# An attention and expert-layer kernel: w_out transposed by DMA, and the softmax reciprocal taken before its broadcast

## The chip, the cores and the metric

The kernel runs on one Trainium2 chip, on all eight of its cores, one launch. Each core takes one of eight sequences and does the same work on it; the cores exchange nothing. The metric is the device time in microseconds (us) of the slowest core.

## The reference, cut to what matters

For each sequence, x is 2048 x 1024. It is normalised, and two branches read the result: attention with 16 heads of 64 under a causal mask, and four expert layers of which each token takes two. Both are added to x. The change touches attention alone:

```python
xn = _layernorm(x, axis=-1)
qkv = jnp.einsum('bse,fe->bsf', xn, w_qkv)          # w_qkv: 3072 x 1024
scores = jnp.einsum('bhqd,bhkd->bhqk', q, k) * scale
scores = jnp.where(causal, scores, -1e30)
attn = jax.nn.softmax(scores, axis=-1)
out = jnp.einsum('bhqk,bhkd->bhqd', attn, v)
out = out.transpose(0, 2, 1, 3).reshape(B, S, E)
a = jnp.einsum('bse,fe->bsf', out, w_out)           # w_out: 1024 x 1024
y = x + a + experts(xn)
```

The sum in the softmax is divided out last: the kernel computes exp(score - 8) without normalising, multiplies by V extended by a column of ones, so that the 65th row of the result is the sum, and then multiplies the other 64 rows by the reciprocal of that row.

## The kernel before

The program is written engine by engine with semaphores set by hand. `I(engine, semaphore, fn)` adds an instruction that raises a semaphore, `E` one that doesn't, and `W` a wait; each engine runs its own list in the order in which the code emits it. `P.brk()` closes a block: all engines meet at a barrier there. Ahead of the first block proper stand small loads and constants; then come four blocks.

**Block with layernorm, Q, K and V (from L249).** GpSimd waits until two quarters of x have landed and then issues three DMA transfers (L253) that read w_qkv in thirds, K first, cast it to bf16 and write it to `wqkv_bf` in DRAM; nothing waits between them. SyncE loads x in four quarters (L331) and then issues 24 DMA transposes (L339), 128 rows each, from `wqkv_bf` to `wqkvT`; the first of each eight waits for its third's cast (SCB1, SCB0, SCB2), and each waits for the transpose before it (SQT). VectorE and ScalarE do layernorm by quarters (`emit_ln`), TensorE transposes the normalised x (L409) and does Q, K (`emit_qk_tt`, L270) and V (`emit_v`, L304). The first K matmul waits for the first transpose.

**Attention block (from L508).** First w_out: for each of eight groups of 128 rows SyncE loads it in f32 (L514), TensorE transposes eight 128x128 tiles (L521), and VectorE copies each to `w_outT` in bf16 (L526). On ScalarE 16 small activations give the gates of the experts (L534); VectorE finishes the gates (L538 to L548) behind its 64 copies, TensorE transposes them (L556), VectorE copies the results (L559), and the first score matmul waits for the last of these copies.

Then the loop over four query tiles `qt` of 512 rows, and in each over eight head pairs. Tile `qt` has `npair` = 2, 4, 6 or 8 steps; a step p of one head is 256 keys:

- `emit_pair`: two score matmuls (L648, L654) into P45 or P67, Exp over both (L662) into `p_sb`, and in the last two steps of a head a mask multiply on VectorE (L670);
- `emit_av`: two matmuls of `p_sb` with V (L683, L690) that add into one of three PSUM slots. The first of a head waits until the multiply with the reciprocal has freed its slot.

The normalising of a head is put off. `flush_stage1` (L609) copies the sum row out of PSUM after a pair's last step. `flush_stage2` has the rest: a matmul with 64 ones broadcasts the row over 64 partitions into `RBP` (L619), ScalarE takes Ln (L623) and Exp of the negative (L627), and VectorE multiplies into `attn_cat` (L633). For the first head of a pair ("the younger head" in the text, of the pair just finished) stage 2 is emitted in the next pair's loop, right behind the first `emit_av`:

```python
            for p in range(npair):
                emit_av(qt, h0, p, npair, u0, s0, a0)
                if p == 0 and pending[0] is not None:
                    flush_stage2(pending[0])
                if p + 1 < npair:
                    emit_pair(qt, h0, p + 1, npair, u0, s0)
                emit_av(qt, h1, p, npair, u1, s1_, a1)
```

For the second head of a pair it is emitted only after the next pair's loop ("the older head"). So at a change of head pair TensorE has, in order: last `emit_av`, the older head's broadcast, two `emit_pair`, `emit_av` of the first head, the younger head's broadcast, `emit_pair`, `emit_av` of the second head. At the end of a tile both heads of the last pair are flushed one after the other. The out-projection of a tile (L715, L720) is spread over the next tile's first head pair; only it reads `w_outT`. Its result goes by way of `proj` to `attn_sc` (L728, L735). In the last tile GpSimd loads expert weights: one load after the fourth head pair, three more (L579, L571, L579) after the last `emit_av`.

**Expert block** (`emit_h` L814, `emit_y` L843): matmuls 128x512 without a gap. **Last block**: x, the attention result and the expert sum are added and stored.

## Time and profile before

| | us |
|---|---|
| median of three runs (3300.23, 3302.22, 3564.77) | 3302.22 |
| the profiled execution | 3302.43 |
| its span, slowest core (the eight: 3288.4 to 3300.9) | 3300.9 |
| block with layernorm, Q, K, V ends | 368 |
| first score matmul | 404.2 |
| expert layers start | 1298.3 |
| TensorE busy | 2867.4 (87%) |
| ScalarE busy | 861.1 (26%) |
| VectorE busy | 752.0 (23%) |

The span is from the first to the last instruction on the slowest core; the execution's own time is 1.5 us longer. In the rows PE is TensorE's matmul, PEld its weight load, ACT ScalarE, DVE VectorE, POOL GpSimd, and SP or SPq SyncE and its DMA queue.
### The profile page before, as it was taken

The page shows a single profiled execution, that of the slowest core. Times are in us where ns is not written, and L with a number is a line of the kernel's source. Part 1 is how long each engine was busy: PE and PEld are TensorE (multiplying, and loading weights), DVE is VectorE, ACT ScalarE, POOL GpSimd, SP SyncE. Part 2 cuts the span into 40 slices and gives each one's busy share as a digit, 9 for nine tenths or more (in the row PEclk, how much of TensorE's full clock was granted, in tenths as well). Part 3 has the DMA queues.
Part 4 walks back from the last instruction along what each step waited for, and adds up shares of the span by engine and source line. Part 5 has one row for each costly group of instructions (what it writes and reads, how often), then busy time and mean ns, then how long its engine had stood idle before and what let it go on. Part 6 is the DMA issues. An engine that isn't in the chain of part 4 may idle for free. (4 is left out here: it accounts for less than half of the span.)

```text
span 3300.9 us, 30637 instructions; the slowest of 8 cores (3288.4 to 3300.9 us)
## 1 busy us (share of the span) xinstructions
PE 2867.4 (87%) x11396; PEld 1146.4 (35%) x11396; DVE 752.0 (23%) x1048; ACT 861.1 (26%) x1164; POOL 35.2 (1%) x59
## 2 busy tenths in 40 slices
PE   3689757778878885999999999999999999999970
PEld 2364301111111112444444444444444444444420
DVE  4521432221121111111111111111111121111224
ACT  1122144545545552112222111112222211211100
POOL 0000000000000000000000000000000000000000
PEclk9769756565565557999999999999999999999955
DMA  9400100000000106032033123303321330230017
GB/s 157 89 10 1 52 0 26 1 26 0 0 26 0 26 0 102 1 51 40 12 52 52 16 36 51 52 1 52 52 29 23 52 52 7 45 51 1 1 49 256
DMA packets 72295, 127.89 MB, mean 39 GB/s; under 512 B 27798, under 2 KB 27926, under 8 KB 71962
## 3 DMA queue, kind: packets, MB, share of 16 engines
q0 software_dynamic: 33520, 73.40, 15.4%
q1 hardware_dynamic: 38634, 52.53, 5.1%
q8 instruction: 98, 1.61, 0.2%
q14 instruction: 43, 0.35, 0.0%
HBM read 176.26 MB, written 23.07 MB: 60 GB/s over the span
## 5 line engine op out<-in xcount | busy, mean ns | idle before, releaser
L814 PE MATMUL P<-xn_fm,w1g 128*128 128x512 bf16 x4096 | 896.9, 380 | 27.6 <-PEq L43 27.6
L843 PE MATMUL P<-w2g,h_sb 128*128 128x512 bf16 x4096 | 894.3, 379 | 0.0
L822 ACT ACTIVATE h_sb<-P,b_sb 128x512 bf16<-128x512 f32 x512 | 352.4, 688 | 1444.9 <-PE P L814 1444.9
L862 DVE SCALAR_TENSOR_TENSOR accum<-P,agate,accum 128x1024 f32<-128x1024 f32 x240 | 308.1, 1284 | 1379.8 <-PE P L843 1379.8
L814 PEld LDWEIGHTS P<-xn_fm,w1g 128*128 128x128 bf16 x4096 | 400.1, 98 | 515.8 <-issue 37.9
L843 PEld LDWEIGHTS P<-w2g,h_sb 128*128 128x128 bf16 x4096 | 400.7, 98 | 483.4
L662 ACT ACTIVATE p_sb<-P,cneg 128x1024 bf16<-128x1024 f32 x320 | 352.0, 1110 | 324.5 <-PE P L654 324.1
L683 PE MATMUL P<-p_sb,v_ext 128*65 128x512 bf16 x320 | 191.6, 599 | 153.4 <-DVE p_sb L670 69.5
L690 PE MATMUL P<-p_sb,v_ext 128*65 128x512 bf16 x320 | 194.8, 609 | 0.0
L683 PEld LDWEIGHTS P<-p_sb,v_ext 128*65 128x65 bf16 x320 | 41.1, 128 | 408.7 <-issue 407.3
L670 DVE TENSOR_TENSOR p_sb<-p_sb,masks 128x1024 bf16<-128x1024 bf16 x128 | 87.9, 690 | 407.1 <-ACT p_sb L662 407.1
L654 PE MATMUL P<-q_fm,k_fm 64*128 64x512 bf16 x320 | 175.7, 609 | 0.0
L648 PE MATMUL P<-q_fm,k_fm 64*128 64x512 bf16 x320 | 168.6, 583 | 7.2 <-DVE proj L728 6.5
L270 PE MATMUL P<-xn_fm,wqkvT 128*128 128x512 bf16 x448 | 117.2, 405 | 25.8 <-DMA wqkvT<-wqkv_bf 16.4
L648 PEld LDWEIGHTS P<-q_fm,k_fm 64*128 64x128 bf16 x320 | 29.0, 99 | 208.6 <-issue 208.6
L633 DVE TENSOR_TENSOR attn_cat<-P,rb 64x512 bf16<-64x512 f32 x64 | 43.7, 683 | 179.1 <-ACT rb L627 173.7
L409 PE MATMUL P<-ident,xnf 128*128 128x128 f32 x128 | 34.4, 406 | 47.3 <-ACT xnf L400 44.9
L270 PEld LDWEIGHTS P<-xn_fm,wqkvT 128*128 128x128 bf16 x448 | 45.5, 103 | 86.3 <-issue 40.7
L715 PE MATMUL P<-w_outT,attn_cat 128*128 128x512 bf16 x240 | 64.8, 431 | 10.4 <-ACT p_sb L662 7.9
L623 ACT ACTIVATE rln<-P 64x512 f32<-64x512 f32 x64 | 37.8, 591 | 120.8 <-PE P L619 120.2
L438 PE MATMUL P<-wr_sb,xfm 128*128 128x4 f32 x256 | 53.0, 339 | 13.8 <-DVE xfm L428 13.8
L438 PEld LDWEIGHTS P<-wr_sb,xfm 128*128 128x128 f32 x256 | 52.0, 310 | 17.7 <-issue 17.7
(106 smaller groups left out, 1019.4 us busy)
## 6 DMA issues: line engine op xcount, KB each, us to landing
w1g<-w POOLq DMA_DIRECT2D x16, 2048.0 KB, 19.5
w2g<-w POOLq DMA_DIRECT2D x16, 2048.0 KB, 30.2
xA<-x SPq DMA_DIRECT2D x4, 2048.0 KB, 31.6
attn_sc<-proj SPq DMA_DIRECT2D x16, 512.0 KB, 2.8
xrg<-x SPq DMA_DIRECT2D x4, 2048.0 KB, 10.8
arg<-attn_sc SPq DMA_DIRECT2D x4, 2048.0 KB, 16.0
y<-outr SPq DMA_DIRECT2D x16, 512.0 KB, 2.8
wqkv_bf<-w_qkv POOLq DMA_DIRECT2D x3, 2048.0 KB, 43.6
```

The source lines that it names most:

```text
L270: t.matmul(pt[:, off:off + 512], wqkvT[:, dc * 3072 + fc8 * 128:dc * 3072 + (fc8 + 1) * 128], xn_fm[:, dc * 2048 + tt * 512:dc * 2048 + (t ...
L438: E("tensor", lambda t, dc=dc, trp=trp: t.matmul(trp[:, 0:4], xfm[:, dc * 128:(dc + 1) * 128], wr_sb[:, dc * 4:(dc + 1) * 4], start=(dc == ...
L648: E("tensor", lambda t, kb0=kb0, pb=pb, hr=hr, pair=pair, qt=qt: t.matmul(pb[:, 0:512], k_fm[hr:hr + 64, pair * 2048 + kb0 * 128:pair * 20 ...
L654: t.matmul(pb[:, 512:1024], k_fm[hr:hr + 64, pair * 2048 + (kb0 + 1) * 128:pair * 2048 + (kb0 + 2) * 128], q_fm[hr:hr + 64, pair * 2048 + ...
L662: ve = I("scalar", "SS", lambda s, pb=pb, psb=psb: s.activation(psb[:], pb[:, 0:1024], AF.Exp, bias=cneg8[:, 0:1]))
L670: vm = I("vector", "SV", lambda v, psb=psb, j=j: v.tensor_tensor(psb[:], psb[:], masks[:, j * 1024:(j + 1) * 1024], ALU.mult))
L683: E("tensor", lambda t, p=p, head=head, psb=psb, sl=sl: t.matmul(sl[0:65, :], bass.AP(v_ext, 2 * p * VW + head * 65, [[NTS * VW, 128], [1, ...
L690: psb=psb, sl=sl, av_stop=av_stop: t.matmul(sl[0:65, :], bass.AP(v_ext, (2 * p + 1) * VW + head * 65, [[NTS * VW, 128], [1, 65]]), psb[:, ...
L814: t.matmul(PH67[par][:, 0:512], w1g[buf][:, dc * 1024 + hc * 128:dc * 1024 + (hc + 1) * 128], xn_fm[:, dc * 2048 + tt * 512:dc * 2048 + (t ...
L822: s.activation(h_sb[tt % 2][:, hc * 512:(hc + 1) * 512], PH67[par][:, 0:512], AF.Gelu, bias=b1_sb[:, e_ * 32 + g_ * 8 + hc:e_ * 32 + g_ * ...
L843: pt=pt, st=st, sp=sp: t.matmul(pt[:, half * 512:(half + 1) * 512], h_sb[tt % 2][:, hc * 512 + ts4 * 128:hc * 512 + (ts4 + 1) * 128], w2g[ ...
L862: v.scalar_tensor_tensor(accum[:, tsg * 1024:(tsg + 1) * 1024], pt[:, 0:1024], agate[:, tsg * 4 + e_:tsg * 4 + e_ + 1], accum[:, tsg * 102 ...
```

## The change

**w_out.** GpSimd casts `w_out` to a bf16 copy in DRAM (`wout_bf`) with a fourth DMA behind the three of w_qkv. In the attention block SyncE waits for it (SCW) and issues eight DMA transposes straight into `w_outT`. The loads, TensorE's 64 transposes and VectorE's 64 copies are gone. Each out-projection waits for the last of the eight (SQW).

**Normalising.** `flush_stage1` now keeps the sum row in f32. In `flush_stage2` ScalarE takes Ln and Exp of that one row, 1x512; TensorE broadcasts the reciprocal row with f32 ones (an f32 matmul in place of a bf16 one); VectorE copies the 64x512 result from `RBP` to `rbsb` and then multiplies. TensorE's broadcast thus waits for ScalarE (SS) and for VectorE's last copy out of `RBP` (SV), where it waited for the row's copy and for ScalarE's last read of `RBP`. The buffers move in SBUF.

```diff
--- before.py
+++ after.py
@@ -62,6 +62,7 @@
     y_h = nc.dram_tensor("y", [S, D], F32, kind="ExternalOutput")
     attn_sc = nc.dram_tensor("attn_sc", [S, D], F32, kind="Internal")
     wqkvbf_h = nc.dram_tensor("wqkv_bf", [3 * D, D], BF16, kind="Internal")
+    woutbf_h = nc.dram_tensor("wout_bf", [D, D], BF16, kind="Internal")
 
     base = (nc.sbuf_base + 31) // 32 * 32
 
@@ -107,8 +108,6 @@
     cm05 = at("cm05", [128, 1], F32, 20416)
 
     xn_fm = at("xn_fm", [128, NDC * S], BF16, 20480)
-    wost0 = at("wost0", [128, 1024], F32, 180736)
-    wost1 = at("wost1", [128, 1024], F32, 184832)
     w_outT = at("w_outT", [128, 8192], BF16, 188928)
     b2_sb = at("b2_sb", [4, 1024], F32, 20480)
     g4_sb = at("g4_sb", [4, 1024], F32, 24576)
@@ -141,12 +140,14 @@
     attn_cat = at("attn_cat", [128, 4096], BF16, 152064)
     p_sb0 = at("p_sb0", [128, 1024], BF16, 160256)
     p_sb1 = at("p_sb1", [128, 1024], BF16, 162304)
-    rb0 = at("rb0", [64, 512], BF16, 164352)
-    rb1 = at("rb1", [64, 512], BF16, 165376)
-    rrow0 = at("rrow0", [1, 512], BF16, 166400)
-    rrow1 = at("rrow1", [1, 512], BF16, 167424)
-    rln0 = at("rln0", [64, 512], F32, 168448)
-    rln1 = at("rln1", [64, 512], F32, 170496)
+    rrow0 = at("rrow0", [1, 512], F32, 164352)
+    rrow1 = at("rrow1", [1, 512], F32, 166400)
+    rln0 = at("rln0", [1, 512], F32, 168448)
+    rln1 = at("rln1", [1, 512], F32, 170496)
+    rbr0 = at("rbr0", [1, 512], F32, 180736)
+    rbr1 = at("rbr1", [1, 512], F32, 182784)
+    rbsb0 = at("rbsb0", [64, 512], F32, 184832)
+    rbsb1 = at("rbsb1", [64, 512], F32, 186880)
     proj0 = at("proj0", [128, 1024], F32, 172544)
     proj1 = at("proj1", [128, 1024], F32, 176640)
 
@@ -170,7 +171,7 @@
     ctx = contextlib.ExitStack()
     sem = {n: ctx.enter_context(nc.semaphore(n))
            for n in ("SX", "SQ0", "SQ1", "SW0", "SW1", "SW2", "SW3", "SXR", "SAR",
-                     "SP0", "SP1", "SEA", "ST", "SV", "SS", "SO", "SG", "SCB0", "SCB1", "SCB2", "SQT")}
+                     "SP0", "SP1", "SEA", "ST", "SV", "SS", "SO", "SG", "SCB0", "SCB1", "SCB2", "SCW", "SQW", "SQT")}
     C = {n: 0 for n in sem}
     P = _Plan()
 
@@ -253,6 +254,7 @@
         I("gpsimd", "SCB%d" % g_, lambda g, g_=g_: g.dma_start(
             wqkvbf_h.ap()[g_ * 1024:(g_ + 1) * 1024, :],
             wqkv_h.ap()[g_ * 1024:(g_ + 1) * 1024, :]), 16)
+    I("gpsimd", "SCW", lambda g: g.dma_start(woutbf_h.ap(), wout_h.ap()), 16)
     slots = [(P01, 0), (P01, 512), (P23, 0), (P23, 512)]
     slot_guard = [("SV", 0)] * 4
     slot_i = 0
@@ -506,28 +508,11 @@
     emit_v(1, tr_evac_chunk[23] + v_xnq[3] + v_ssq[3])
 
     P.brk()
-    wost = [wost0, wost1]
-    v_wo_trlast = [0] * 8
+    W("sync", "SCW", 16)
     for fc in range(8):
-        if fc >= 2:
-            W("sync", "ST", v_wo_trlast[fc - 2])
-        v_dma = I("sync", "SQ%d" % (fc % 2), lambda e, fc=fc: e.dma_start(
-            wost[fc % 2][:], wout_h.ap()[fc * 128:(fc + 1) * 128, :]), 16)
-        W("tensor", "SQ%d" % (fc % 2), v_dma)
-        for i in range(NDC):
-            trp = TRS[tr_idx % 4]
-            if tr_idx >= 4:
-                Wtr("tensor", tr_evac[tr_idx - 4])
-            v_t = I("tensor", "ST", lambda t, fc=fc, i=i, trp=trp: t.transpose(
-                trp[0:128, 0:128], wost[fc % 2][:, i * 128:(i + 1) * 128],
-                ident[:]))
-            v_wo_trlast[fc] = v_t
-            W("vector", "ST", v_t)
-            v_ev = I("vector", "SV", lambda v, fc=fc, i=i, trp=trp: v.tensor_copy(
-                w_outT[:, i * 1024 + fc * 128:i * 1024 + (fc + 1) * 128],
-                trp[0:128, 0:128]))
-            tr_evac[tr_idx] = v_ev
-            tr_idx += 1
+        v_sqw = I("sync", "SQW", lambda e, fc=fc: e.dma_start_transpose(
+            bass.AP(w_outT, fc * 128, [[8192, 128], [1024, 8], [1, 128]]),
+            woutbf_h.ap()[fc * 128:(fc + 1) * 128, :]), 16)
 
     v_ex_last = 0
     for ts in range(NTS):
@@ -586,9 +571,10 @@
         return emit_w2_dma(i)
 
     p_sb = [p_sb0, p_sb1]
-    rb = [rb0, rb1]
     rrow = [rrow0, rrow1]
     rln = [rln0, rln1]
+    rbr = [rbr0, rbr1]
+    rbsb = [rbsb0, rbsb1]
     proj = [proj0, proj1]
     PB = [P45, P67]
     SLOT = [P23[:, 0:512], P23[:, 512:1024], P01[:, 0:512]]
@@ -613,26 +599,30 @@
         nonlocal rb_guard
         head, pair, hr, qt_, v_r = pend[0], pend[1], pend[2], pend[3], pend[5]
         sl = SLOT[slot_of[head]]
+        W("scalar", "SV", v_r)
+        E("scalar", lambda s, head=head: s.activation(
+            rln[head % 2][0:1, :], rrow[head % 2][0:1, :], AF.Ln))
+        E("scalar", lambda s: s.drain())
+        v_exp = I("scalar", "SS", lambda s, head=head: s.activation(
+            rbr[head % 2][0:1, :], rln[head % 2][0:1, :], AF.Exp,
+            scale=cneg1[0:1, 0:1]))
         gs, gv = rb_guard
         W("tensor", gs, gv)
-        W("tensor", "SV", v_r)
+        W("tensor", "SS", v_exp)
         v_rb = I("tensor", "ST", lambda t, head=head: t.matmul(
-            RBP[0:64, :], ones_bf[0:1, 0:64],
-            rrow[head % 2][0:1, :], start=True, stop=True))
-        W("scalar", "ST", v_rb)
-        v_ln = I("scalar", "SS", lambda s, head=head: s.activation(
-            rln[head % 2][:], RBP[0:64, :], AF.Ln))
-        rb_guard = ("SS", v_ln)
-        E("scalar", lambda s: s.drain())
-        v_exp = I("scalar", "SS", lambda s, head=head: s.activation(
-            rb[head % 2][:], rln[head % 2][:], AF.Exp, scale=cneg1[0:64, 0:1]))
-        W("vector", "SS", v_exp)
+            RBP[0:64, :], ones_f[0:1, 0:64],
+            rbr[head % 2][0:1, :], start=True, stop=True))
+        W("vector", "ST", v_rb)
+        v_rc = I("vector", "SV", lambda v, head=head: v.tensor_copy(
+            rbsb[head % 2][:], RBP[0:64, :]))
+        rb_guard = ("SV", v_rc)
+        E("vector", lambda v: v.drain())
         if qt_ > 0:
             W("vector", "ST", v_outproj[qt_ - 1])
         v_am = I("vector", "SV", lambda v, head=head, pair=pair, hr=hr, sl=sl:
                  v.tensor_tensor(
                      attn_cat[hr:hr + 64, pair * 512:(pair + 1) * 512],
-                     sl[0:64, :], rb[head % 2][:], ALU.mult))
+                     sl[0:64, :], rbsb[head % 2][:], ALU.mult))
         att_guard[slot_of[head]] = ("SV", v_am)
         v_attnmult_last[0] = v_am
 
@@ -701,6 +691,7 @@
     def emit_opuser(qt_src, ts4):
         bpar = ts4 % 2
         pb = PB[bpar]
+        W("tensor", "SQW", v_sqw)
         gs, gv = sc_guard[bpar]
         W("tensor", gs, gv)
         if ts4 == 0:
```

The order on the engines, at the places that matter. GpSimd's queue, from the start of the layernorm block; `wqkv_bf` and `wout_bf` are the bf16 copies in DRAM, `w1g`, `w2g` the expert weights. Before:

```order
L43 UNCONDITIONAL_BRANCH
L47 UNCONDITIONAL_BRANCH [waits barrier_Pool_Activation_PE_DVE_SP_gather]
L253 DMA wqkv_bf<-w_qkv 64x16384 [waits SXR,SAR]
L253 DMA wqkv_bf<-w_qkv 64x16384 x2
L43 UNCONDITIONAL_BRANCH
L47 UNCONDITIONAL_BRANCH [waits barrier_Pool_Activation_PE_DVE_SP_gather]
L571 DMA w1g_102<-w 128x8x1024 [waits ST]
L579 DMA w2g_104<-w 128x8x1024 [waits ST]
```

and with the change:

```order
L43 UNCONDITIONAL_BRANCH
L47 UNCONDITIONAL_BRANCH [waits barrier_Pool_Activation_PE_DVE_SP_gather]
L254 DMA wqkv_bf<-w_qkv 64x16384 [waits SXR,SAR]
L254 DMA wqkv_bf<-w_qkv 64x16384 x2
L257 DMA wout_bf<-w_out 64x16384
L43 UNCONDITIONAL_BRANCH
L47 UNCONDITIONAL_BRANCH [waits barrier_Pool_Activation_PE_DVE_SP_gather]
L556 DMA w1g_100<-w 128x8x1024 [waits ST]
```

One transfer has come in behind the three, with no wait of its own.

VectorE's queue, from the start of the attention block; `exa` to `agate` are the gates, `aem` their transpose. Before:

```order
L526 CAST w_outT<-P 128x128 [waits ST] x64
L538 TENSOR_TENSOR g2a<-exa,mask_68 128x64 [waits SS]
L541 TENSOR_REDUCE Sa<-g2a 128x1 x16
L544 RECIPROCAL rSa<-Sa 128x16
L548 TENSOR_SCALAR agate<-g2a,rSa 128x4 x16
L559 COPY aem<-P 4x128 [waits ST] x16
```

and with the change:

```order
L523 TENSOR_TENSOR g2a<-exa,mask_68 128x64 [waits SS]
L526 TENSOR_REDUCE Sa<-g2a 128x1 x16
L529 RECIPROCAL rSa<-Sa 128x16
L533 TENSOR_SCALAR agate<-g2a,rSa 128x4 x16
L544 COPY aem<-P 4x128 [waits ST] x16
L660 TENSOR_TENSOR p_sb_114<-p_sb_114,masks 128x1024 [waits SS]
```

The 64 copies ahead of the gates are gone; the rest stands in the same order.

TensorE's queue at the first change of head pair in the second query tile that has both broadcasts (`rrow` or `rbr` with the ones); it starts with the last `emit_av` of a pair. Before:

```order
L683 MATMUL P<-p_sb_117,v_ext 65x512 [waits SV]
L690 MATMUL P<-p_sb_117,v_ext 65x512
L619 MATMUL P<-rrow_121,ones_bf 64x512 [waits SS,SV]
L648 MATMUL P<-q_fm,k_fm 128x512 [waits SS]
L654 MATMUL P<-q_fm,k_fm 128x512
L648 MATMUL P<-q_fm,k_fm 128x512 [waits SS]
L654 MATMUL P<-q_fm,k_fm 128x512
L683 MATMUL P<-p_sb_116,v_ext 65x512 [waits SS,SV]
L690 MATMUL P<-p_sb_116,v_ext 65x512
L619 MATMUL P<-rrow_120,ones_bf 64x512 [waits SS,SV]
L648 MATMUL P<-q_fm,k_fm 128x512 [waits SS]
```

and with the change:

```order
L673 MATMUL P<-p_sb_115,v_ext 65x512 [waits SV]
L680 MATMUL P<-p_sb_115,v_ext 65x512
L612 MATMUL P<-rbr_121,ones_f 64x512 [waits SV,SS]
L638 MATMUL P<-q_fm,k_fm 128x512 [waits SS]
L644 MATMUL P<-q_fm,k_fm 128x512
L638 MATMUL P<-q_fm,k_fm 128x512 [waits SS]
L644 MATMUL P<-q_fm,k_fm 128x512
L673 MATMUL P<-p_sb_114,v_ext 65x512 [waits SS,SV]
L680 MATMUL P<-p_sb_114,v_ext 65x512
L612 MATMUL P<-rbr_120,ones_f 64x512 [waits SV,SS]
L638 MATMUL P<-q_fm,k_fm 128x512 [waits SS]
```

The broadcasts stand where they stood. SS and SV in their waits now mean ScalarE's Exp of the row and VectorE's copy out of `RBP`; before they meant ScalarE's Ln of the head before and VectorE's row copy.

ScalarE's queue at a change of head pair (here in the first tile; the others read alike); `p_sb` are the Exps of scores. Before:

```order
L662 ACTIVATE p_sb_116<-P,cneg_47 128x1024 [waits ST]
L662 ACTIVATE p_sb_117<-P,cneg_47 128x1024 [waits ST]
L623 ACTIVATE rln_123<-P 64x512 [waits ST]
L627 ACTIVATE rb_119<-rln_123,cneg_77 64x512
L662 ACTIVATE p_sb_116<-P,cneg_47 128x1024 [waits ST]
L662 ACTIVATE p_sb_117<-P,cneg_47 128x1024 [waits ST]
```

and with the change:

```order
L652 ACTIVATE p_sb_114<-P,cneg_47 128x1024 [waits ST]
L652 ACTIVATE p_sb_115<-P,cneg_47 128x1024 [waits ST]
L603 ACTIVATE rln_119<-rrow_117 1x512 [waits SV]
L606 ACTIVATE rbr_121<-rln_119,cneg_77 1x512
L652 ACTIVATE p_sb_114<-P,cneg_47 128x1024 [waits ST]
L652 ACTIVATE p_sb_115<-P,cneg_47 128x1024 [waits ST]
```

The order is the same. Ln waits for VectorE's row (SV) where it waited for TensorE's broadcast (ST), and both work on one partition.

## Rows read from the trace of the kernel before

**Rows 1.** Stretches: window, length, busy us of PE PEld DVE ACT POOL, clock, DMA

```profile
1040.00:1140.00 100.00, 87.56 (x184) 14.21 (x183) 14.41 (x22) 55.19 (x56) 0.92 (x1) 0.50 0.16 21
3165.00:3170.00 5.00, 5.00 (x7) 2.00 (x6) 1.56 (x2) 0.00 (x0) 0.00 (x0) 0.50 0.00 0
```

**Rows 2.** Timeline, attention starts; columns: start us, us, instruction, idle before

```profile
369.34 3.14 ACT L534 ACTIVATE exa<-lgt,nm1a 128x4 f32<-128x4 f32 x16
...
396.13 0.22 DVE L538 TENSOR_TENSOR g2a<-exa,mask 128x64 f32<-128x64 f32 x1
...
404.22 0.71 PE L648 MATMUL P<-q_fm,k_fm 64*128 64x512 bf16 x2 [0.53 <-DVE aem L559]
```

**Rows 3.** Timeline, a change of head pair in the second query tile

```profile
590.25 0.63 PE L619 MATMUL P<-rrow,ones_bf 1*64 1x512 bf16 x1
...
590.98 0.59 ACT L623 ACTIVATE rln<-P 64x512 f32<-64x512 f32 x1 [2.63 <-PE P L619]
591.22 0.63 PE L654 MATMUL P<-q_fm,k_fm 64*128 64x512 bf16 x2
...
592.28 2.09 ACT L662 ACTIVATE p_sb<-P,cneg 128x1024 bf16<-128x1024 f32 x2
592.54 0.69 DVE L633 TENSOR_TENSOR attn_cat<-P,rb 64x512 bf16<-64x512 f32 x1 [3.40 <-ACT rb L627]
593.26 1.29 DVE L609 CAST rrow<-P 1x512 bf16<-1x512 f32 x2
...
593.62 0.61 PE L683 MATMUL P<-p_sb,v_ext 128*65 128x512 bf16 x1 [1.77 <-ACT p_sb L662]
...
594.59 0.63 PE L619 MATMUL P<-rrow,ones_bf 1*64 1x512 bf16 x1
...
597.71 0.61 PE L683 MATMUL P<-p_sb,v_ext 128*65 128x512 bf16 x1 [1.53 <-DVE attn_cat L633]
...
601.03 0.63 PE L654 MATMUL P<-q_fm,k_fm 64*128 64x512 bf16 x1
...
601.82 1.11 ACT L662 ACTIVATE p_sb<-P,cneg 128x1024 bf16<-128x1024 f32 x1 [0.84 <-PE P L654]
```

**Rows 4.** Timeline, the f32 matmuls of one row in the last block

```profile
3140.30 3.57 PE L951 MATMUL P<-csum_sb,ones_f 1*4 1x512 f32 x4 [1.57 <-DVE csum_sb L946]
```

**Rows 5.** Timeline, a change of head pair in the first query tile

```profile
426.93 0.63 PE L619 MATMUL P<-rrow,ones_bf 1*64 1x512 bf16 x1
...
431.09 1.27 DVE L670 TENSOR_TENSOR p_sb<-p_sb,masks 128x1024 bf16<-128x1024 bf16 x2
...
436.03 0.61 PE L683 MATMUL P<-p_sb,v_ext 128*65 128x512 bf16 x1 [1.46 <-DVE attn_cat L633]
```

**Rows 6.** Timeline, end of the first query tile

```profile
512.71 0.63 PE L619 MATMUL P<-rrow,ones_bf 1*64 1x512 bf16 x1
...
516.48 0.60 PE L619 MATMUL P<-rrow,ones_bf 1*64 1x512 bf16 x1 [3.14 <-DVE rrow L609]
...
520.02 1.09 ACT L662 ACTIVATE p_sb<-P,cneg 128x1024 bf16<-128x1024 f32 x1
```

**Rows 7.** Line L579 from 1000 to 1300 us, then the timeline where the expert layers start

```profile
L579 POOL DMA_DIRECT2D w2g<-w x2: 886/890/893, 1246.9 to 1248.6; - x2
...
DMA to landing us min/median/max: 18.0/33.4/48.9
...
1298.25 2.29 PE L814 MATMUL P<-xn_fm,w1g 128*128 128x512 bf16 x5 [27.57 <-PEq L43]
```

**Rows 8.** Lines L253, then L339, then the timeline before the first K matmul

```profile
L253 POOL DMA_DIRECT2D wqkv_bf<-w_qkv x3: 498/521/677, 25.4 to 26.6; - x3
...
DMA to landing us min/median/max: 24.4/43.6/63.6
...
DMA to landing us min/median/max: 3.0/3.3/46.3
...
96.69 3.15 PE L270 MATMUL P<-xn_fm,wqkvT 128*128 128x512 bf16 x7 [14.93 <-DMA wqkvT<-wqkv_bf]
```

## The prediction

> **What bounds the kernel now.** I first read the table of stretches, then the timeline where the change sits, then the DMA answers. The program has four blocks: layernorm with Q, K and V up to 368 us, attention from 368 to about 1298, the expert layers to 3145, the end. The expert layers take 1850 us and hold no edit. Of attention the reader should see [rows 1]: in the fourth query tile TensorE is busy 87.6 of 100 us at a granted clock of 0.50 (the 1.2 GHz level), ScalarE 55.2. So there TensorE's queue, in order, sets the time, and whatever is put into it or makes it wait is paid. At the start of the block the reader should see how late VectorE takes up what ScalarE has ready [rows 2]; at a change of head pair, a chain over three engines [rows 3]; before the first K matmul, a wait for a DMA transpose [rows 8].
>
> **Part 1, w_out is transposed by DMA.** This removes eight loads, 64 TensorE transposes and 64 copies. ScalarE's 16 small activations start at 369.34 and take 3.14 us, so their result is there at 372.5. Today VectorE takes it up at 396.13, behind its 64 copies, and the first score matmul follows 8.09 us later, at 404.22 [rows 2]. Without the copies the same chain starts at about 372.6. Gain: 396.13 - 372.6 = 23.5 us. The eight new DMA transposes stand on SyncE's queue ahead of the first store of an out-projection, each waits for the one before, and each takes about 3.3 us [rows 8]: 26 us in all. The first reader of w_outT comes after the first query tile's last broadcasts (512.71 [rows 6]), over 100 us on, and that hides them; if it did not, up to 26 us would be added.
>
> The cast of w_out to bf16 is a fourth transfer behind the three of w_qkv on GpSimd's queue, and it is not free. The three were issued from 25.4 to 26.6 us and landed after 24.4, 43.6 and 63.6 us, thus at 49.8, 69.6 and 90.2: 20 us each [rows 8]. The first transpose of w_qkv was issued as soon as the first cast had landed, at 49.8. It took 46.3 us where the median one takes 3.3, and landed at 96.1, six microseconds after the last cast. TensorE waited 14.93 us for it, until 96.69 [rows 8]. I read this as: a transfer of SyncE makes almost no way while casts are in flight. A fourth cast of the same size ends at 90.2 + 20.6 = 110.8, the first transpose lands at about 116.6, and TensorE starts Q and K 20.5 us later. VectorE's layernorm work that fills this wait is already done by then, so nothing takes the delay up. Bounds: nothing, if transposes make way between the casts' packets, and 21 us. I take 20.5, the row's own pattern.
> By the Trainium skill, "DMA: Bandwidth & Descriptors", section "Issuing engines are not separate DMA queues", transfers from different engines run on the same DMA engines and interleave. Taken evenly, that would let the first transpose through during the casts and make this term about 3 us; the row of 46.3 us speaks against an even share.
>
> **Part 2, the reciprocal before the broadcast.** Today: row copy (VectorE), broadcast of one bf16 row over 64 partitions (TensorE), Ln and Exp on 64x512 (ScalarE), multiply (VectorE). New: row copy, Ln and Exp on 1x512, broadcast of an f32 row, copy out of PSUM, multiply. The longer row of the chain does not get shorter on fewer partitions: two 1x512 row copies take 1.29 us where one 64x512 multiply takes 0.69 [rows 3]. So Ln and Exp keep their price, about 1.6 us from the start of Ln to the reader of Exp (590.98 to 592.54) [rows 3].
>
> The f32 broadcast itself: the nearest rows are f32 matmuls of one row by 512 columns. Two calls show four records, together 3.57 us, thus 0.85 us from start to start [rows 4], and the f32 stretch at 3165 us is at clock 0.50 [rows 1], attention's own level. A broadcast is then 1.71 us in place of 0.43, plus 1.28. Bounds: 0.43 (one pass) and 1.71. I take 1.71.
>
> Now the chain at a change of head pair, with t = 0 at the broadcast of the older head, 590.25 [rows 3]. Today: second score matmul at 0.97 (591.22), Exp of scores at 2.03, attention-times-V (AV) of the first head at 3.37, broadcast of the younger head at 4.34, AV of the second head at 7.46 (597.71), after the multiply that frees its PSUM slot. With the change:
> - the older head's Ln and Exp now wait for no matmul and are done beforehand; its broadcast starts at 0. The second score matmul starts at 0.97 + 1.28 = 2.25, Exp of scores 0.79 later (601.03 to 601.82), at 3.04, so AV of the first head is at 4.38: 1.01 later;
> - ScalarE finishes both Exps of scores (2.09 us) at 5.13. Behind them in its queue stand Ln and Exp of the younger head: result at 5.13 + 1.6 = 6.7. TensorE reaches its broadcast at 4.38 + 0.97 = 5.35 and waits 1.35 us. Queued behind the waiting matmul are the scores and AV of both heads, and on VectorE the copy and the multiply;
> - broadcast from 6.7, second record's end at 6.7 + 0.85 + 1.06, copy 0.1 later at 8.7 (0.68 us), multiply (0.68 us), handovers 0.2: AV of the second head at 10.3 against 7.46, **2.8 us**.
> From there on TensorE is the bound [rows 1], so it stays. Such a change occurs six times in each query tile; 18 times in tiles 2 to 4: 50.4 us.
>
> In the first tile the masks lengthen the chain: from 426.93 the first mask is at 4.16 and AV of the second head at 9.10 [rows 5]. New: copy, multiply and two row copies end at 2.01 + 0.68 + 0.06 + 0.68 + 0.04 + 1.29 = 4.76, the mask is 0.6 late; TensorE then reaches the younger broadcast at 6.65, ScalarE at 6.7, no wait; from there to AV 3.58 in place of 3.12: 1.15 us, six times, 6.9 us.
> The first change in each tile has only the younger broadcast: 1.35 + 0.46 = 1.8 us, three times, and about 1 in the first tile: 6.4 us.
> At a tile's end three broadcasts stand in a row, and nothing covers Ln and Exp: from 512.71 the second is at 3.77 and the next tile's Exp of scores at 7.31 [rows 6]. New: the multiply is 0.46 later, the row is ready at 4.3, Exp at 5.9, second broadcast 5.9, its copy ends at 8.6, third broadcast 8.7 (it writes the PSUM the copy reads), scores from 8.7 + 1.85, Exp of scores at 11.7: 4.4 us, three times, 13.2 us. At the fourth tile's end this costs nothing: the expert layers started at 1298.25, 0.8 us after the last of three weight loads landed (issued 1248.6, 48.9 us) [rows 7]; these are issued once the last AV is done, ahead of the broadcasts.
> Part 2: 50.4 + 6.9 + 6.4 + 13.2 = 76.9 us.
>
> **Sum.** 20.5 - 23.5 + 76.9 = 73.9 us onto the profiled execution's 3302.4 us (span 3300.9): 3376.3. Its time is the median of the runs shown (3302.2) within 0.2 us. That is 2.2% slower; 2%, 66 us, is about what a measurement can tell.
>
> **Rivals.**
> 1. *The casts let the transposes through.* For it: they share engines, not a queue. Against: 46.3 us [rows 8]. Part 1 then gains 20: 3376 - 17 = 3359.
> 2. *The f32 broadcast is cheap.* For it: in that row four records serve two calls, and their second halves may be short when one matmul stands alone. Against: 3.57 us for four [rows 4]. At 0.85 per broadcast 64 x 0.85 = 54 us less, some of it hidden: about 3326.
> 3. *The clock rises (faster than before).* TensorE's added work fills its gaps, attention gets the 2.4 GHz level, and ScalarE becomes the bound. In the fourth tile 87.6 busy us would halve to 44 and ScalarE's 55.2 decide: 40 us per 100, 120 us over the tile's 300. Time: 3256. [...] Against: the f32 stretch is busy 5.00 of 5.00 us at 0.50 [rows 1], so a full TensorE with thin operands did not rise.
> By the Trainium skill, "TensorE: Matmul & The Clock Gate", section "Why this matters for your kernels", keeping TensorE continuously busy brings the full clock; that would give this rival's time. The row at 3165 us does not follow it.
> 4. *The block's start does not get shorter*, because attention waits for more than the gates, so that the change does not do what it says there. For it: 35 us lie between the first activation and the first score matmul. Against: the multiply at 396.13 is late by its own queue alone [rows 2], and the only reader of w_outT is the out-projection. Without the gain: 3376 + 23.5 = 3400.
>
> **How the numbers follow.** Forecast (3362 to 3392 its own range, from 1.4 to 1.8 us for Ln and Exp and handovers of 0 to 0.3 us at 24 places): 0.72. Rival 1: 0.14. Rival 2: 0.09. Rival 3: 0.03. Rival 4: 0.02. The range 3340 to 3398 leaves out rivals 2 to 4. Slower by over 2% (above 3368): 0.66 of the forecast's 0.72, 0.02 of rival 1 and rival 4, together 0.70; within 2%: 0.27; faster: 0.03.
>
> **What would show it.** First transpose of w_qkv landing near 116 us with TensorE waiting about 35 us for it; first score matmul 12 us after the block's start; two broadcast records of about 1.06 us per head, 128 in all; a wait of TensorE on Exp of the younger head, about 1.3 us, some 20 times; attention's last AV about 74 us later; expert layers as long as before. I am wrong if K starts at 97 us, if the broadcast takes 0.43 us, or if attention shows a granted clock over 0.6 outside the out-projections.

## The result, and the profile after

| | before | after |
|---|---|---|
| median of the runs, us | 3301.9 (10 runs) | 3391.7 (9 runs) |
| ratio, 95% interval | | 1.0231 (1.0198 to 1.0265) |
| spans of the eight cores, us | 3288.4 to 3300.9 | 3360.0 to 3390.1 |

The change makes the kernel slower by 2.3%; the prediction was 2.2%, 3376 us in a range of 3340 to 3398. Some runs had a lower granted clock on some cores, and these are in the medians but not in the ratios; the profiled execution of after (3391.7 us) has a little of it on cores 2 and 3, with 0.81 for a while in the Q and K matmuls, which took 233 us there and 215 to 218 us on the other six. Taken through the ratio, after is at 1.0231 x 3301.9 = 3378 us. I read after on core 7, the core that the rows of before are from; the longest of the other five has a span of 3375.0 us.

Milestones on core 7, in us:

| | before | after | shift so far |
|---|---|---|---|
| first K matmul | 96.7 | 116.3 | +19.6 |
| V ends | 366.6 | 387.0 | +20.4 |
| first score matmul | 404.2 | 401.1 | -3.1 |
| last attention-times-V (AV) matmul | 1245.7 | 1323.0 | +77.3 |
| last broadcast of attention | 1251.6 | 1332.5 | +80.9 |
| expert layers start | 1298.2 | 1373.7 | +75.5 |
| expert layers end | 3126.8 | 3202.3 | +75.5 |
| span ends | 3300.9 | 3370.8 | +69.9 |

On the six cores other than 2 and 3 the start of the expert layers moved by 70.7 to 77.7 us, 75.2 in the mean. The last block came out 5.6 us shorter on core 7, but that is this core's spread and not the change: from the end of the expert layers to the end of the span the eight cores took 165.0 to 174.1 us before and 164.3 to 172.7 after, 169.2 and 168.5 in the mean, and core 7 of before is the longest of all.

The stretches of after (columns as in [rows 1]), the first two in the fourth query tile, the third in the last block's f32 matmuls:

```profile
1060.00:1160.00 100.00, 89.57 (x180) 14.27 (x178) 14.27 (x21) 52.20 (x51) 0.00 (x0) 0.50 0.00 0
1160.00:1260.00 100.00, 85.52 (x170) 13.56 (x168) 19.68 (x29) 50.32 (x52) 0.92 (x1) 0.50 0.13 21
3230.00:3260.00 30.00, 30.00 (x36) 11.62 (x35) 11.02 (x9) 0.00 (x0) 0.00 (x0) 0.50 0.00 0
```

In the fourth tile TensorE is about as busy as before and the clock is still 0.50: it did not rise. ScalarE, at 50 to 52 us of 100, has fallen a little, since attention as a whole takes longer.

The start of Q and K on core 7, as [rows 8]: the timeline's row of the first K matmul, then the transposes of w_qkv with the landing times of their DMAs, the casts of w_qkv, and the cast of w_out:

```profile
116.26 3.02 PE L272 MATMUL P<-xn_fm,wqkvT 128*128 128x512 bf16 x7 [31.37 <-DMA wqkvT<-wqkv_bf]
```

```profile
L341 SPq DMA_TRANSPOSE wqkvT<-wqkv_bf x24: 1217/1218/56477, 53.8 to 192.5; - x24
DMA to landing us min/median/max: 3.1/3.3/61.9
...
L254 POOL DMA_DIRECT2D wqkv_bf<-w_qkv x3: 498/521/675, 28.0 to 29.2; - x3
DMA to landing us min/median/max: 25.8/45.6/65.6
...
L257 POOL DMA_DIRECT2D wout_bf<-w_out x1: 498/498/498, 29.7 to 29.7; - x1
DMA to landing us min/median/max: 83.2/83.2/83.2
```

The fourth cast lands at 29.7 + 83.2 = 112.9. The first transpose, issued at 53.8, lands at 53.8 + 61.9 = 115.7, and TensorE starts at 116.3 after waiting 31.4 us.

The start of attention on core 7, as [rows 2]:

```profile
389.80 3.11 ACT L519 ACTIVATE exa<-lgt,nm1a 128x4 f32<-128x4 f32 x16
393.01 0.23 DVE L523 TENSOR_TENSOR g2a<-exa,mask 128x64 f32<-128x64 f32 x1 [4.79 <-ACT exa L519]
...
401.12 0.71 PE L638 MATMUL P<-q_fm,k_fm 64*128 64x512 bf16 x2 [0.53 <-DVE aem L544]
```

VectorE takes up ScalarE's result 0.1 us after it is there, where it had been 23.6 us late, and the same chain of 8.1 us follows. From the end of V to the first score matmul it is 14.1 us in place of 37.6.

The head-pair change in tile 2 on core 7, the place of [rows 3]:

```profile
605.73 1.96 PE L612 MATMUL P<-rbr,ones_f 1*64 1x512 f32 x2
607.63 0.61 PE L638 MATMUL P<-q_fm,k_fm 64*128 64x512 bf16 x2
...
608.81 2.12 ACT L652 ACTIVATE p_sb<-P,cneg 128x1024 bf16<-128x1024 f32 x2 [3.68 <-PE P L644]
...
610.17 0.61 PE L673 MATMUL P<-p_sb,v_ext 128*65 128x512 bf16 x1 [1.51 <-DVE rrow L595]
...
610.82 0.61 ACT L603 ACTIVATE rln<-rrow 1x512 f32<-1x512 f32 x1
611.50 0.72 ACT L606 ACTIVATE rbr<-rln,cneg 1x512 f32<-1x512 f32 x1
612.36 1.93 PE L612 MATMUL P<-rbr,ones_f 1*64 1x512 f32 x2 [1.16 <-ACT rbr L606]
...
614.40 0.68 DVE L616 COPY rbsb<-P 64x512 f32<-64x512 f32 x1 [3.75 <-PE P L612]
615.25 0.68 DVE L623 TENSOR_TENSOR attn_cat<-P,rbsb 64x512 bf16<-64x512 f32 x1 [0.16 <-issue]
...
616.07 0.61 PE L673 MATMUL P<-p_sb,v_ext 128*65 128x512 bf16 x1 [0.82 <-DVE attn_cat L623]
```

From the older head's broadcast (605.73) the Exp of scores is at 3.08, AV of the first head at 4.44, the younger head's broadcast at 6.63, AV of the second head at 10.34; the prediction had 3.04, 4.38, 6.7 and 10.3, and before the last of them was 7.46. Each broadcast is now two records (x2) and the next matmul starts 1.90 us after it. Before it was 0.57 us, from the broadcast at 590.25 [rows 3] to this row of before:

```profile
590.82 0.61 PE L648 MATMUL P<-q_fm,k_fm 64*128 64x512 bf16 x2
```

An f32 broadcast thus holds TensorE for 1.33 us more.

The end of the first tile on core 7, as [rows 6]:

```profile
518.03 1.96 PE L612 MATMUL P<-rbr,ones_f 1*64 1x512 f32 x2
...
523.93 1.93 PE L612 MATMUL P<-rbr,ones_f 1*64 1x512 f32 x2 [3.94 <-ACT rbr L606]
...
526.91 1.93 PE L612 MATMUL P<-rbr,ones_f 1*64 1x512 f32 x2 [1.04 <-DVE rbsb L616]
...
529.96 2.12 ACT L652 ACTIVATE p_sb<-P,cneg 128x1024 bf16<-128x1024 f32 x2 [4.86 <-PE P L644]
```

The three broadcasts and the next tile's first Exp of scores stand at 0, 5.90, 8.88 and 11.93; predicted were 5.9, 8.7 and 11.7.

### The profile page after: what moved, and what is told of

It is laid out like the page before. It is cut to its first block and busy times, and to the rows that moved or that the text cites. A ratio compares the mean times of both kernels' runs of the same rounds, so it can differ in the third digit from the quotient of the medians.

```text
span 3390.1 us, 30384 instructions; the slowest of 8 cores (3360.0 to 3390.1 us)
## 1 busy us (share of the span) xinstructions
PE 2939.8 (87%) x11204; PEld 1149.1 (34%) x11396; DVE 780.6 (23%) x1048; ACT 861.0 (25%) x1164; POOL 35.6 (1%) x60
## 5 line engine op out<-in xcount | busy, mean ns | idle before, releaser
L272 PE MATMUL P<-xn_fm,wqkvT 128*128 128x512 bf16 x436 | 129.5, 444 | 47.3 <-DMA wqkvT<-wqkv_bf 35.4
L612 PE MATMUL P<-rbr,ones_f 1*64 1x512 f32 x128 | 124.7, 1075 | 45.8 <-ACT rbr L606 41.7
L616 DVE COPY rbsb<-P 64x512 f32<-64x512 f32 x64 | 43.7, 683 | 208.8 <-PE P L612 208.8
```

The source lines that it names most:

```text
L272: t.matmul(pt[:, off:off + 512], wqkvT[:, dc * 3072 + fc8 * 128:dc * 3072 + (fc8 + 1) * 128], xn_fm[:, dc * 2048 + tt * 512:dc * 2048 + (t ...
L612: v_rb = I("tensor", "ST", lambda t, head=head: t.matmul(RBP[0:64, :], ones_f[0:1, 0:64], rbr[head % 2][0:1, :], start=True, stop=True))
```

## The experiments

Each kernel ran beside the kernel before; ratios and their 95% intervals are to be read as in the table above.

**Part 1 alone, and part 2 alone.** The first is before with the diff's w_out part, the second is after with the eight loads, 64 transposes and 64 copies of w_out back (their two buffers share the memory of `rbr` and `rbsb`, which are written only later).

```diff
r1_dma_wout, against before
+    I("gpsimd", "SCW", lambda g: g.dma_start(woutbf_h.ap(), wout_h.ap()), 16)
...
-            v_t = I("tensor", "ST", lambda t, fc=fc, i=i, trp=trp: t.transpose(
...
-            v_ev = I("vector", "SV", lambda v, fc=fc, i=i, trp=trp: v.tensor_copy(
...
+        v_sqw = I("sync", "SQW", lambda e, fc=fc: e.dma_start_transpose(
...
r2_recip_only, against after: the same lines with + and - exchanged
```

> Part 1 alone: w_out cast and transposed by DMA as in the change, normalising as before. Theory (a fourth cast holds the first transpose of w_qkv back): the first K matmul is 20 us later than before, at about 116 us, the first score matmul 23.5 us nearer to the block's start, together 3 us faster, 3299 against 3302. Rival (the cast costs nothing on the path, the change's 74 us are all of part 2): K at 97 us, 3279.

> Part 2 alone: Ln and Exp on one row, f32 broadcast, copy out of PSUM; w_out as before. Theory: 77 us slower than before, 3379; from the first score matmul to the last broadcast 85 us more than before's 847. Rival (part of the 85 us in attention comes from the DMA transposes of w_out that run beside it): at most 60 us slower, and attention 10 or more us shorter than with the whole change.

Part 1 alone: 3299.3 us, ratio 0.9993 (0.9972 to 1.0015). The first K matmul was at 114.0 to 117.5 on the eight cores, the first score matmul on core 7 at 400.7, and from there to the last broadcast it took 845.8 us, as before (847.4). Its loss of 20 and its gain of 23.5 cancel. Part 2 alone: 3382.1 us, ratio 1.0236 (1.0195 to 1.0276); the first K matmul at 95.9 on core 7, and attention took 931.9 us from its first score matmul to its last broadcast, as with the whole change (931.4), so w_out's transposes beside it cost it nothing. So the whole slowdown is part 2, and part 1 hides a gain under a loss.

**The cast alone.** Before, with a fourth cast whose copy nobody reads; then with a fifth.

```diff
r3_cast_only, against before
+    I("gpsimd", "SCW", lambda g: g.dma_start(woutbf_h.ap(), wout_h.ap()), 16)
r9_two_casts, against r3_cast_only
+    I("gpsimd", "SQW", lambda g: g.dma_start(woutbf2_h.ap(), wout_h.ap()), 16)
```

> The kernel before with the fourth cast added and its result read by nobody. Theory: the first transpose lands near 116 us, K starts 20 us later, and the time is 20 us longer, 3322. Rival (the delay is made up for in the layernorm block or is the eight later transposes' doing): under 8 us longer.

> The kernel before with two more casts that nobody reads, five in all. Theory (each cast in front of the first transpose adds its own length): the first transpose lands near 137 us, K starts 40 us later than before, and the time is 38 to 41 us longer, 3340. Rival (one more cast falls into a gap, or x's last quarter has got through by then so that the transposes follow before the casts end): K at 125 us or earlier, under 30 us longer.

The profiled executions took 3320.7 and 3334.6 us, 18 and 32 us over before's 3302.4; over the runs of before that go into a ratio beside them (3299.6 and 3298.3 in the median) it is 18 to 21 and 36 us. The first K matmul of the second, on core 7:

```profile
134.55 3.14 PE L274 MATMUL P<-xn_fm,wqkvT 128*128 128x512 bf16 x7 [50.45 <-DMA wqkvT<-wqkv_bf]
```

With three, four and five casts in flight the first transpose landed 46.3 [rows 8], 61.6 and 80.2 us after its issue, and K began at 96.7, 117.1 and 134.6. The last cast landed at 90.2, 113.7 and 131.4, so the fourth took 18.7 us and the fifth 18.0: each cast costs about its own length once more. The fifth came out a little below what I expected (K 37.9 us later and not 40, the time 36 and not 38 to 41). That TensorE's wait follows the casts, in these three steps, is shown; why the transposes wait for them is not, only that they do.

**The casts out of the way.** Part 1 with w_out's cast issued only after all 24 transposes of w_qkv; then also the casts of Q and V held back until the eight K transposes have landed; and, the other way about, before with x's last quarter loaded behind those eight.

```diff
r6_late_cast, against r1_dma_wout: the cast of w_out behind the last transpose of w_qkv
+    W("gpsimd", "SQT", v_tq)
+    I("gpsimd", "SCW", lambda g: g.dma_start(woutbf_h.ap(), wout_h.ap()), 16)
r8_k_first, against r6_late_cast
     for g_ in (1, 0, 2):
+        if g_ == 0:
+            W("gpsimd", "SQT", 128)
r7_x4_after_k, against before: in the loop over the transposes
+        if g_ == 1:
+            emit_x(3)
```

> Part 1 alone, with the cast of w_out issued only once all 24 transposes of w_qkv have landed. Theory: K starts at 97 us as before, the gain at the start of attention stays, 3279. Rival (the casts' delay comes from the DMA engines' total load, or the late cast disturbs attention's start): 3295 or more.

> As r6_late_cast, and the casts of the Q and V thirds of w_qkv wait until the eight K transposes have landed. Theory (a transpose makes no way while any cast is in flight): the first transpose lands within 10 us of the first cast, K starts as soon as TensorE has done its layernorm work, near 82 us instead of 97, and the time is 14 us below r6_late_cast, 3265. Rival (the transpose is held by the last quarter of x that stands ahead of it in SyncE's queue): it lands later than 60 us and K gains under 5 us.

> The kernel before, with the load of x's last quarter issued behind the eight K transposes instead of ahead of them; the three casts as before. Theory A (casts in flight starve whatever SyncE has issued): the first transpose still lands only when the third cast has, at 90 us or later, K starts at 92 to 97 us, and the time is within 5 us of before. Theory B (the transpose is slow because x's last quarter stands ahead of it in the same queue, and only that long row of packets is starved): the first transpose lands by 65 us, K starts near 83 us, and the time is 5 to 10 us below before (the third quarter's layernorm comes out from under the wait).

With the late cast: 3281.2 us, ratio 0.9948 (0.9932 to 0.9964), K at 94 to 98 and the first score matmul at 380: part 1 without its loss, a gain of 17 to 19 us. With K's transposes first: 3272.6 us, ratio 0.9915 (0.9899 to 0.9931). K began at 82.2, 14 us earlier, but only about 9 us of it arrived at the end, so the 3265 that I expected was missed by 6 to 8 us: the matmuls of Q and K then took 221 us in place of 215. The timeline of that kernel on core 7:

```profile
82.10 1.01 POOL L256 DMA_DIRECT2D wqkv_bf<-w_qkv  x2 [56.03 <-DMA wqkvT<-wqkv_bf]
82.24 3.15 PE L273 MATMUL P<-xn_fm,wqkvT 128*128 128x512 bf16 x7 [0.73 <-DVE lgt L451]
...
99.11 1.58 PE L415 MATMUL P<-ident,xnf 128*128 128x128 f32 x5 [7.40 <-ACT xnf L406]
```

The first K matmul waits for no DMA any more. Seventeen microseconds later TensorE waits 7.4 us for the next piece of layernorm (`xnf`), which before was done while TensorE waited for the transpose. I had taken it that nothing would be late next there; the next thing was.

The transposes of the same kernel show both sides of the rule. The first K transpose, with no other cast in flight, and the first Q transpose, with the cast of V in flight:

```profile
L342 SPq DMA_TRANSPOSE wqkvT<-wqkv_bf x1: 1690/1690/1690, 49.8 to 49.8; - x1
DMA to landing us min/median/max: 7.2/7.2/7.2
...
L342 SPq DMA_TRANSPOSE wqkvT<-wqkv_bf x1: 1637/1637/1637, 101.7 to 101.7; - x1
DMA to landing us min/median/max: 19.3/19.3/19.3
```

The first landed at 57.0, as I had expected (under 10 us), 1.1 us after x's last quarter, which stood ahead of it on SyncE's queue (10.3 + 45.6 = 55.9). The second landed at 121.0, 0.9 us after the cast of V (82.6 + 37.5 = 120.1).

The third kernel parts the casts from x's quarter. With x's quarter behind the transposes and all three casts in flight, the first transpose, issued at 52.4, landed at 90.2, 1.0 us after the last cast (28.9 + 60.3 = 89.2), where before it had been 5.9 us after it [rows 8]. K began at 90.7 on core 7 and the time was 3291.9 to 3293.1 us, 6 us under the kernel before. Of my two theories the first had the transpose right (at 90 us or later) and K and the time just outside its limits (92 us, 5 us); the second is refuted, for it had the transpose land by 65 us. So of before's wait the casts hold it up to 90.2 us, and about 5 of the last 6 us are x's quarter, which itself landed only at 95.1, 1.0 us ahead of the transpose.

**What the price of part 2 is.** Before, with only the broadcast made f32 (row copy and ones in f32, Ln and Exp behind it as before); and after, with the reciprocal row and the ones in bf16, so that the f32 matmul alone is gone (a lower precision of the reciprocal than the change has).

```diff
r5_f32_only, against before
-    rrow0 = at("rrow0", [1, 512], BF16, 166400)
+    rrow0 = at("rrow0", [1, 512], F32, 180736)
-            RBP[0:64, :], ones_bf[0:1, 0:64],
+            RBP[0:64, :], ones_f[0:1, 0:64],
r4_after_bf16, against after
-    rbr0 = at("rbr0", [1, 512], F32, 180736)
+    rbr0 = at("rbr0", [1, 512], BF16, 180736)
-            RBP[0:64, :], ones_f[0:1, 0:64],
+            RBP[0:64, :], ones_bf[0:1, 0:64],
```

> The kernel before with one thing changed: the sum row is kept and broadcast in f32 (two records of 0.85 us for one of 0.43); Ln, Exp and multiply stay where they were, behind the broadcast. If the extra 1.28 us of a broadcast enter the chain of a head-pair change twice: 2 x 1.28 x 24, 4 x 1.28 and 3 x 3.8 us at the tiles' ends, 78 us, 3380: then the f32 matmul is all of part 2's price and the new order of Ln and Exp is free. Rival (TensorE's wait for Exp, 1.35 us a time, is a part of its own, as the prediction's sum has it): about 45 us, 3347.

> The whole change, but the reciprocal row and the ones are bf16, so that the broadcast is one pass of 0.43 us; Ln and Exp of one row ahead of it, the copy and the f32 sum row stay. Theory (the f32 passes are all of part 2's price): a head-pair change in tiles 2 to 4 costs about what it did (AV of the second head at 7.6 to 7.8 after the older broadcast, against 7.46), TensorE still waits about 1.3 us for the younger head's Exp, the first tile's changes get about 1 us shorter; attention as long as before within 8 us, 3300. Rival (the wait for Exp and the added copy cost by themselves): 3325 or more.

f32 alone: 3383.0 us, ratio 1.0238 (1.0204 to 1.0272), as much as all of part 2. The whole change in bf16: 3305.4 us in the median of ten runs, 3292.0 at the lowest, ratio 1.0000 (0.9982 to 1.0017), attention on core 7 846.3 us. The groups of the broadcast over the whole kernel, each on its slowest core: first before itself, then f32 alone, then the whole change in bf16:

```profile
L619 PE MATMUL P<-rrow,ones_bf 1*64 1x512 bf16 x64 | 39.9, 623 | 16.5 <-DVE rrow L609 12.8 <-ACT rln L623 3.8
```

```profile
L619 PE MATMUL P<-rrow,ones_f 1*64 1x512 f32 x128 | 123.6, 1066 | 16.5 <-DVE rrow L609 12.8 <-ACT rln L623 3.8
```

```profile
L612 PE MATMUL P<-rbr,ones_bf 1*64 1x512 bf16 x64 | 39.4, 615 | 46.0 <-ACT rbr L606 41.8 <-DVE rbsb L616 4.2
```

and the same of after itself (from the page, core 2):

```profile
L612 PE MATMUL P<-rbr,ones_f 1*64 1x512 f32 x128 | 124.7, 1075 | 45.8 <-ACT rbr L606 41.7
```

These rows are the lesson of the case. The kernel with bf16 idles 46.0 us ahead of its broadcasts, 41.8 of it for ScalarE's reciprocal, as after does, and in sum loses nothing. The one with f32 alone idles 16.5 us, as before does, and has all of the slowdown. So the 29.5 us of new idle time are not the price. The timelines of the two on core 7 at a head-pair change in tile 2, f32 alone:

```profile
593.40 1.97 PE L619 MATMUL P<-rrow,ones_f 1*64 1x512 f32 x2
...
598.11 0.61 PE L683 MATMUL P<-p_sb,v_ext 128*65 128x512 bf16 x1 [1.77 <-ACT p_sb L662]
...
599.07 1.96 PE L619 MATMUL P<-rrow,ones_f 1*64 1x512 f32 x2
...
603.52 0.61 PE L683 MATMUL P<-p_sb,v_ext 128*65 128x512 bf16 x1 [1.53 <-DVE attn_cat L633]
```

and the whole change in bf16:

```profile
599.38 0.63 PE L612 MATMUL P<-rbr,ones_bf 1*64 1x512 bf16 x1
...
604.68 0.60 PE L612 MATMUL P<-rbr,ones_bf 1*64 1x512 bf16 x1 [1.16 <-ACT rbr L606]
...
607.06 0.61 PE L673 MATMUL P<-p_sb,v_ext 128*65 128x512 bf16 x1 [0.82 <-DVE attn_cat L623]
```

From the older broadcast to AV of the second head: 7.46 us before [rows 3], 7.68 in bf16 with the new order, 10.12 with f32 alone, 10.34 with both. The f32 broadcast lies on this chain twice, 2 x 1.33 = 2.66 us, and the new order adds 0.22. In the new order TensorE idles 1.16 us ahead of the younger broadcast, but behind it stand a copy and a multiply on VectorE where Ln, Exp and a multiply stood: the wait is little more than Ln and Exp moved ahead of the matmul.

That the new order costs nothing in sum is a balance of two signs. The first tile of the whole change in bf16 on core 7, the place of [rows 5]:

```profile
422.36 0.63 PE L612 MATMUL P<-rbr,ones_bf 1*64 1x512 bf16 x1
...
425.81 1.27 DVE L660 TENSOR_TENSOR p_sb<-p_sb,masks 128x1024 bf16<-128x1024 bf16 x2
...
430.04 0.61 PE L673 MATMUL P<-p_sb,v_ext 128*65 128x512 bf16 x1 [0.75 <-DVE attn_cat L623]
```

AV of the second head is at 7.68 after the older broadcast, where it was at 9.10: with no Ln and Exp between broadcast and multiply the masks start 0.71 us earlier, and the second half gains as much again. From one older broadcast to the next the first tile takes 12.85 us in place of 14.30, six times, which gives back 8.7 us; I had expected about 1 us a time. The 18 later changes cost 0.20 to 0.23 us each, 3.8 in all; the three crossings from tile to tile and the end of the last tile cost 4.1, and the start of the first tile gives back 0.3. Together it is 1.1 us less: 846.3 for 847.4. Under the f32 broadcast the new order costs about 2 us: on cores 0, 1, 4, 6 and 7 attention takes 928.0 to 930.6 us with f32 alone and 930.1 to 931.7 in after.

**A version that beats both.** After with the bf16 row and the DMA order of the kernel with K's transposes first.

> r8_k_first's DMA order together with r4_after_bf16's normalising. Theory: the two do not touch each other, so r8_k_first plus what r4_after_bf16 is above or below r1_dma_wout: 3265 within 8 us. Rival (they share ScalarE's or VectorE's slack): over 3275.

It took 3267.5 us (four runs, 3265.2 to 3273.8), ratio 0.9910 (0.9894 to 0.9925): 1% under before. Its gain comes from part 1 and the order of the casts; before's own normalising with the same DMA order stood at 0.9915, which the intervals do not tell from 0.9910.

## Why the prediction was right, and where its working was not

- **The casts (predicted +20.5).** Measured +19.6 on core 7, and with the cast alone +20.4 for K and 18 to 21 us in the time. The rule I read out of one row, that a transfer of SyncE makes almost no way while casts are in flight, held for the transposes with four and five casts; for a plain load it was too wide, since x's third quarter landed at 57.6 us (9.8 + 47.8), between the first two casts. The size is nearer than its parts: the third cast landed 4.6 us later than before (94.8 for 90.2), the fourth took 18.1 us and not 20.6, and the first transpose came 2.8 us behind it and not 5.9. These errors nearly cancel.
- **The start of attention (-23.5).** Measured -23.5 (37.6 to 14.1 us), and the eight w_out transposes, 3.4 us each, were done about 120 us before the first out-projection (412.5 + 3.4 = 415.9, and 535.2).
- **The head-pair change.** 2.88 us against 2.8 in tiles 2 to 4. In the first tile the mask is at 4.78 and AV of the second head at 10.34, against 4.76 and 10.25. (The 3.12 us that the prediction took for the first tile's stretch behind the younger broadcast are the second tile's; it was 3.05 there, which changes nothing.)
- **The tile's end.** 11.93 against 11.7. That the fourth's costs nothing was right: its last broadcast came 9.5 us after the last AV in place of 5.9, but from the last AV to the expert layers it took 50.7 us in place of 52.6.
- **The sum of part 2 (76.9).** From the first score matmul to the last AV attention grew by 80.4 us (841.5 to 921.9). Read off the older broadcasts on core 7, term by term: 51.7 for the 18 changes of tiles 2 to 4 (predicted 50.4), 7.3 for the six of the first tile (6.9), 20.3 for the three crossings from tile to tile, each the end of one tile and the first change of the next (13.2 + 5.4 = 18.6), and 1.1 at the start of the first tile (1). Half of the missing 3.5 us is in the crossings. Part 2 alone gave 78 to 82 us in the time.
- **What was luck.** The forecast lies 2 us from the 3378 of the ratio because small errors of both signs meet: attention 3.5 us over its sum, the casts 0.9 under, the way from the last AV to the expert layers 1.9 shorter, where the sum had nothing. A spread of 7 us between cores at the start of the expert layers says how much such closeness is worth.
- **The step that failed.** The working had the 2.8 us as 1.01 for the older broadcast, 1.35 for TensorE's wait on Exp, 0.46 behind it. The sum was right and the reasons half wrong: the experiments give 1.33 for each of the two f32 broadcasts and 0.22 for everything else. Whoever had acted on my working would have moved Ln and Exp back behind the broadcast to be rid of the wait. That kernel is f32 alone, and it is as slow as the whole change (1.0238 and 1.0231); the lever was the type of the broadcast's two operands. I made the mistake by walking along one chain only. Each step was true of the kernel with both edits, but a step's length there is not what its edit costs, since the wait replaces work that stood behind the matmul before.
- **Rival 1** (the casts let transposes through) fell: K began at 116.3, not 97. The Trainium skill, "DMA: Bandwidth & Descriptors", section "Issuing engines are not separate DMA queues", says that transfers from different engines interleave on the same DMA engines; here a transpose of SyncE took 46.3, 61.6 and 80.2 us behind three, four and five casts, so an even share was not what this traffic got.
- **Rival 2** (f32 is cheap) fell: 128 records of 1.07 us each, 1.90 us from a broadcast to the next matmul.
- **Rival 3** (the clock rises, faster) fell: granted clock 0.50 with TensorE busy 89.6 of 100 us, and 0.50 in the last block with 30.00 of 30.00. The rule of the Trainium skill, "TensorE: Matmul & The Clock Gate", section "Why this matters for your kernels", that keeping TensorE continuously busy brings the full clock, is not what the second of these stretches shows; the first has gaps and cannot decide it.
- **Rival 4** (the block's start is not shorter) fell, by the 14.1 us.

What stays open: by what rule the casts hold the transposes back; and why the crossings from tile to tile took 1.7 us more than forecast.

## What to carry to other kernels

Before a price is put on a new wait, take out of the sum what used to stand behind the waiting instruction and now stands ahead of it; a group's idle time is not what the edit costs, and only a kernel with one of the two edits says which one is paid. Read such a price in every stage: the same new order cost 0.2 us a time in three tiles here and gave back 1.4 in the first. A matmul of one row is not small: in bf16 it took 0.63 us here, as long as one of 64 rows (0.61), and in f32 the next matmul could start only after 1.90 us and not 0.57, 64 times on the engine that bounds the stage. A DMA that "runs in the background" at a kernel's start is not free while others wait for DMAs: put behind the last transfer that TensorE waits for there, the same cast no longer delayed K.

## What the runs showed of the hardware that I had not expected

- How completely casting DMAs of GpSimd's queue held back transposes issued by SyncE: the median transpose lands in 3.3 us, the first one landed 61.9 us after its issue with four casts in flight, and 1.0 us after the last cast once nothing else stood ahead of it. Without a cast in flight the first one took 7.2 us. A plain load was slowed too: x's last quarter landed at 95.1 us with three casts issued and at 55.9 with one. A cast of 4 MB to 2 MB landed 18 to 21 us after the one before it, with three, four or five issued together.
- An f32 matmul of one row over 64 ones took 1.96 us for its two records; two calls with four columns of ones took 3.57 us for four [rows 4], 1.79 us a call. Sixteen times the columns of the other operand hardly mattered.
